# Moving the next step's normalisation, transposes and routing to earlier units in a fused macaron block

## What is computed

```python
x = x + 0.5 * ffn(layernorm(x))
x = x + attention(layernorm(x))
x = x + 0.5 * ffn(layernorm(x))

def ffn(x):                                   # x: tokens x 128
    scores = sigmoid(x @ router_w.T)          # 16 experts in 4 groups
    s = scores + bias
    # the 2 groups with the largest sum of their two best s, in them the 4 best experts
    tw = 2.5 * scores[chosen] / (scores[chosen].sum() + 1e-20)
    h, u = x @ gate_w[e], x @ up_w[e]         # every expert e, F = 128
    y = (silu(h) * u) @ down_w[e]
    return sum_e(combine[:, e] * y[e]) + shared(x)   # shared: two more such products

def attention(x):                             # 32 heads of 4, softmax-free
    q, k, v = split(x @ Wqkv_w.T + Wqkv_b)
    ctx = (q @ k.T) @ v                       # per head
    ctx = groupnorm(ctx per head over time and head dim) * gn_w + gn_b
    return ctx @ out_w.T + out_b
```

## Time and profile before

| | |
|---|---|
| median of 3 runs | 751.8 us (751.61 to 751.99) |
| profiled execution, its own time | 755.5 us |
| its span | 753.8 us |
| mean granted clock of TensorE | 0.965 |
| instructions | 12004 |

### The profile page before, as it was taken

One profiled execution on the slowest core, in us unless ns is written; L12 is line 12 of the kernel. 1 busy time (PEld: TensorE's weight loads), 2 busy tenths in 40 slices (PEclk: granted clock), 3 DMA queues, 4 the chain that ended last, 5 costly groups with the idle time before them and its releaser, 6 DMA issues.

```text
span 753.8 us, 12004 instructions
## 1 busy us (share of the span) xinstructions
PE 680.1 (90%) x3116; PEld 555.4 (74%) x3116; DVE 592.5 (79%) x1571; ACT 397.6 (53%) x784; POOL 432.1 (57%) x373
## 2 busy tenths in 40 slices
PE   3498989989898988989979989799897999989897
PEld 2287778878787877778867878678686878878675
DVE  3898696878887697886878878878788797878674
ACT  3464645555573543755436554366553655555453
POOL 4555655666673553855547455475553766666564
PEclk9799999999998998999989999899998999999999
DMA  6640606041230601405006051050410606041240
GB/s 189 191 168 2 224 1 225 1 180 46 98 129 0 225 2 31 195 0 224 0 5 221 0 194 45 3 223 14 174 65 0 225 15 225 15 168 72 66 174 15
DMA packets 30789, 76.37 MB, mean 101 GB/s; under 512 B 3968, under 2 KB 12688, under 8 KB 30736
## 3 DMA queue, kind: packets, MB, share of 16 engines
q1 hardware_dynamic: 30736, 75.81, 28.0%
HBM read 73.18 MB, written 2.62 MB: 101 GB/s over the span
## 4 chain that ended last, share of the span: by engine, by line
PE 33%; DVE 21%; issue 20%; POOL 18%; DMA 4%; ACT 2%; POOLq 1%; SPq 0%; DVEq 0%; ACTq 0%
POOL A_lo L323 16%; DVE T L952 6%; DVE A L974 5%; PE gateP L410 4%; PE gateP L412 3%; PE gateP L411 3%; PE yP L410 3%; PE yP L411 3%; PE yP L412 3%; PE upP L412 3%; PE upP L411 3%; PE upP L410 3%; DMA CB<-combT 2%; DVE wsum L841 2%; DMA ebias<-in_L_ffn_bias_dram 1%
## 5 line engine op out<-in xcount | busy, mean ns | idle before, releaser
L323 POOL TENSOR_TENSOR A_lo<-A,A_hi 128x512 fp32r<-128x512 f32 x288 | 371.5, 1295 | 252.7 <-ACT A_hi L673 252.6
L656 ACT ACTIVATE gateP<-gateP 128x512 f32<-128x512 f32 x256 | 149.0, 582 | 232.1 <-PE gateP L412 231.6
L952 DVE TENSOR_TENSOR T<-gateP,CB 128x512 f32<-128x512 f32 x256 | 175.3, 685 | 103.9 <-ACT gateP L656 81.1
L673 ACT CAST A_hi<-A 128x512 fp32r<-128x512 f32 x288 | 176.6, 613 | 42.6 <-DVE A L974 42.6
L974 DVE TENSOR_TENSOR A<-upP,T 128x512 f32<-128x512 f32 x256 | 177.0, 691 | 9.1
L410 PE MATMUL gateP<-XT_hi,W_hi 128*128 128x512 f32 x288 | 124.6, 433 | 3.5 <-DVE T L952 3.1
L410 PE MATMUL yP<-A_hi,W_hi 128*128 128x512 f32 x288 | 115.0, 399 | 1.5 <-ACT YT L589 0.9
L410 PE MATMUL upP<-XT_hi,W_hi 128*128 128x512 f32 x288 | 115.5, 401 | 0.3
L412 PE MATMUL gateP<-XT_lo,W_hi 128*128 128x512 f32 x288 | 115.4, 401 | 0.0
L411 PE MATMUL gateP<-XT_hi,W_lo 128*128 128x512 f32 x288 | 115.3, 400 | 0.0
L412 PE MATMUL upP<-XT_lo,W_hi 128*128 128x512 f32 x288 | 114.6, 398 | 0.0
(11 more groups left out here) (169 smaller groups left out, 671.6 us busy)
## 6 DMA issues: line engine op xcount, KB each, us to landing
CB<-combT SPq DMA_DIRECT2D x128, 512.0 KB, 7.1
out_dram<-X SPq DMA_DIRECT2D x8, 256.0 KB, 2.0
X<-in_L_attn_x_dram SPq DMA_DIRECT2D x3, 512.0 KB, 6.1
W_in<-in_L_ffn_gate_w_dram SPq DMA_DIRECT2D x4, 256.0 KB, 5.3
W_in<-in_L_ffn_up_w_dram SPq DMA_DIRECT2D x4, 256.0 KB, 5.3
W_in<-in_L_ffn_down_w_dram SPq DMA_DIRECT2D x4, 256.0 KB, 5.4
X<-in_L_attn_x_dram SPq DMA_DIRECT2D x2, 256.0 KB, 3.7
combT<-CT SPq DMA_DIRECT2D x16, 32.0 KB, 1.8
```

The lines of the kernel that those rows point to most:

```text
L323: pool.tensor_tensor(A_lo[:, slot, :], A[:, slot, :], A_hi[:, slot, :].bitcast(F32), ALU.subtract).then_inc(low_done, 1)
L656: act.activation(dst, gateP[u % 2][:, :], ACT.Silu).then_inc(silu_done, 1)
L673: act.copy(A_hi[:, v % SLOTS, :], A[:, v % SLOTS, :]).then_inc(high_done, 1)
L952: dve.tensor_tensor(T[:, u % TS, :], gateP[u % 2][:, :], CB[:, e, :], ALU.mult).then_inc(gate_weighted, 1)
```

## The change

The preparation is spread over two steps. `stats`, `step_rstd`, `normalise` and `transpose_next` of a step stand at units 12, 13, 14 and 16, and 17 of the step before the preceding one (so they are for step t+2 while step t runs); `next_full` and `next_high` at unit 0, `next_low` and `logits` at unit 1, `route` at units 2 to 9, `route_silu` at 3, `transpose_weights` at 11 and `copy_weights` at 12 of the preceding step. Step 0 prepares step 1 as before (`early`), and step 2 at its units 12 to 17 besides. `transpose_next` gets a further wait, for the copy of the combine weights out of `prepP`. Of attention the stages move three units forward, with some exceptions: statistics take units 0 to 2 in place of 1 to 4, GpSimd's two powers stand at 3 and 27, the `zb` group goes from 31 to 29, the `WoT` product from 32 to 31, its copy from 33 to 32; units 33 to 35 of VectorE and 34 of TensorE stay.

```diff
 pool (GpSimd)
-                    if w == 1 and not (last and s == 1):
-                        step_rstd(2 * p + s + 1)
-                    if w == 7 and not (last and s == 1):
+                    early = first and s == 0
+                    if early and w == 1:
+                        step_rstd(1)
+                    if w == 13 and not last:
+                        step_rstd(2 * p + s + 2)
+                    if w == (7 if early else 1) and not (last and s == 1):
                         next_low(2 * p + s + 1, (s + 1) % 2)
-                    if attention and u == 5:
+                    if attention and u == 3:
...
-                    if attention and u == 30:
+                    if attention and u == 27:

 pe (TensorE)
             def transpose_next(t):
                 pe.wait_ge(xn_ready, 2 * (t + 1))
+                if not (isinstance(t, int) and t == 0):
+                    pe.wait_ge(ct_ready, t)
...
+                    early = first and s == 0
+                    if early and w == 5:
+                        transpose_next(1)
                     if not (last and s >= 1):
-                        if w == 5:
-                            transpose_next(t0 + s + 1)
-                        if w == 7:
+                        if w == (7 if early else 1):
                             logits(t0 + s + 1)
-                        if w == 16:
+                        if w == (16 if early else 11):
                             transpose_weights(t0 + s + 1)
+                    if w == 17 and not last:
+                        transpose_next(t0 + s + 2)
 pe attention: units 12, 15, 16, 19, 21, 23, 26, 29, 32 become 9, 12, 13, 16, 18, 20, 23, 26, 31

 act (ScalarE)
+                    early = first and s == 0
+                    if early and w in (2, 3):
+                        normalise(1, 1, w - 2)
                     if not (last and s >= 1):
-                        if w in (2, 3 if first and s == 0 else 4):
-                            normalise(t0 + s + 1, 2 * ((p + s) % BATCH) + (1 - s), (w - 1) // 2)
-                        if w == 6:
+                        if w == (6 if early else 0):
                             next_high(t0 + s + 1, (s + 1) % 2)
-                        if w == 9:
+                        if w == (9 if early else 3):
                             route_silu(t0 + s + 1)
-                        if w == 17:
+                        if w == (17 if early else 12):
                             copy_weights(t0 + s + 1)
+                    if w in (14, 16) and not last:
+                        normalise(t0 + s + 2, 2 * ((p + 1) % BATCH) + s, w // 2 - 7)
 act attention: units 7 to 10, 13, 16, 22, 33 become 4 to 7, 10, 13, 19, 32

 dve (VectorE)
+                    if early and w == 0:
+                        dve.wait_ge(x_rest, 16 * BATCH)
+                        stats(1, 1)
                     if not (last and s == 1):
...
+                        at = 6 if early else 0
+                        if w == at:
+                            next_full(t0 + s + 1)
+                        if at + 2 <= w < at + 10:
+                            route(t0 + s + 1, w - at - 2)
+                    if w == 12 and not last:
+
+                        dve.wait_ge(mul_done, n + u + 1)
+                        stats(t0 + s + 2, 2 * ((p + 1) % BATCH) + s)
 dve attention: units 1 to 4, 14, 17, 20, 24, 27, 30, 31 become 0 to 2, 11, 14, 17, 21, 24, 27, 29
```

More of the change, by code:

```diff
@@ L449, in attention_stage @@
                 v = ATT_OPS * b
-                if u == 12:
+                if u == 9:
                     pe.wait_ge(xa_ready, b + 1)
@@ L456, in attention_stage @@
                     mm.then_inc(att_pe, 1)
-                if u in (12, 15):
-                    g = (u - 12) // 3
+                if u in (9, 12):
+                    g = (u - 9) // 3
                     if g == 0:
@@ L467, in attention_stage @@
                     mm.then_inc(att_pe, 1)
-                if u == 16:
+                if u == 13:
                     pe.wait_ge(att_act, 6 * b + 1)
@@ L474, in attention_stage @@
                               start=True, stop=True).then_inc(att_pe, 1)
-                if u == 19:
+                if u == 16:
                     pe.wait_ge(att_seq, v + 8)
                     pe.matmul(attP[:, 0:P], WkT[:, :], P1[:, :], start=True, stop=True).then_inc(att_pe, 1)
-                if u == 21:
+                if u == 18:
                     pe.wait_ge(att_seq, v + 10)
@@ L482, in attention_stage @@
                               start=True, stop=True).then_inc(att_pe, 1)
-                if u == 23:
+                if u == 20:
                     pe.wait_ge(att_act, 6 * b + 5)
                     pe.matmul(attP[:, 0:P + 1], Am[:, :], Gc[:, :], start=True, stop=True).then_inc(att_pe, 1)
-                if u == 26:
+                if u == 23:
                     pe.wait_ge(att_seq, v + 12)
@@ L489, in attention_stage @@
                               start=True, stop=True).then_inc(att_pe, 1)
-                if u == 29:
+                if u == 26:
                     pe.wait_ge(att_seq, v + 14)
@@ L493, in attention_stage @@
                               start=True, stop=True).then_inc(att_pe, 1)
-                if u == 32:
+                if u == 31:
                     pe.wait_ge(att_seq, v + 19)
@@ L615, in attention_stage @@
             def attention_stage(u, b):
-                if 7 <= u < 11:
-                    if u == 7:
+                if 4 <= u < 8:
+                    if u == 4:
                         act.wait_ge(att_pow, 3 * b + 2)
-                    for j in range(2 * (u - 7), 2 * (u - 6)):
+                    for j in range(2 * (u - 4), 2 * (u - 3)):
                         ins = act.activation(XA[:, j, 0:P], X[:, bass.ds(b * BT + j, 1), :]
@@ L623, in attention_stage @@
                                              scale=arstd[:, j:j + 1], bias=ashift[:, j:j + 1])
-                    if u == 10:
+                    if u == 7:
                         ins.then_inc(xa_ready, 1)
-                if u == 13:
+                if u == 10:
                     act.wait_ge(att_pe, 12 * b + 1)
                     act.copy(GS[:, :], attP[:, 0:P + 1]).then_inc(att_act, 1)
-                if u in (13, 16):
-                    g = (u - 13) // 3
+                if u in (10, 13):
+                    g = (u - 10) // 3
                     act.wait_ge(att_pe, 12 * b + 2 + g)
                     act.copy(XAT[:, g * TILES:(g + 1) * TILES, :], backP[:, :]).then_inc(att_act, 1)
-                if u == 22:
+                if u == 19:
                     act.wait_ge(att_pe, 12 * b + 6)
@@ L636, in attention_stage @@
                     act.copy(Am[:, :], attP[:, 2 * P:3 * P]).then_inc(att_act, 1)
-                if u == 33:
+                if u == 32:
                     act.wait_ge(att_pe, 12 * b + 10)
@@ L856, in attention_stage @@
                 v = ATT_OPS * b
-                if 1 <= u <= 4:
-                    j0 = 2 * (u - 1)
-                    if u == 1:
+                if u < 3:
+                    if u == 0:
                         dve.wait_ge(x_updated, 2 * b + 2)
-                    for j in (j0, j0 + 1):
+                    for j in range(3 * u, min(3 * u + 3, BT)):
                         ins = dve.bn_stats(ast[:, j, :], X[:, bass.ds(b * BT + j, 1), :]
                                            .rearrange("p o d -> p (o d)"))
-                    if u == 4:
+                    if u == 2:
                         ins.then_inc(att_seq, 1)
                         merge_stats(att_seq, v, ast, anmean[:, :], avar[:, :], aparts)
-                if u == 14:
+                if u == 11:
                     dve.wait_ge(att_act, 6 * b + 1)
@@ L885, in attention_stage @@
                                              ALU.mult, ALU.add).then_inc(att_seq, 1)
-                if u == 20:
+                if u == 17:
                     dve.wait_ge(att_pe, 12 * b + 5)
@@ L899, in attention_stage @@
                                       ALU.add).then_inc(att_seq, 1)
-                if u == 27:
+                if u == 24:
                     dve.wait_ge(att_seq, v + 12)
@@ L914, in attention_stage @@
                                       ALU.add).then_inc(att_seq, 1)
-                if u == 31:
+                if u == 29:
                     dve.wait_ge(att_pow, 3 * b + 3)
@@ L958, in pair @@
                     w, s = u % UNITS, u // UNITS
-                    if w in (13, 14) and not (last and s == 1):
-                        dve.wait_ge(route_seq, ROUTE_OPS * (t0 + s + 1) + (21 if w == 13 else 22))
+                    early = first and s == 0
+                    if w in ((13, 14) if early else (7, 8)) and not (last and s == 1):
+                        dve.wait_ge(route_seq, ROUTE_OPS * (t0 + s + 1) + (21 if w in (7, 13) else 22))
                     dve.wait_ge(silu_done, n + u + 1)
```

6 lines of the change are left out of this document (3 added, 3 removed).

## The result

The changed kernel takes 739.9 us (median of 4 runs, 739.06 to 740.61), the kernel before 751.9 in the same session: a ratio of 0.984 (95% interval 0.982 to 0.986), 12.0 us less. Forecast were 717 us and a range of 706 to 731. The sign was right, the gain a third of the forecast one. The profiled execution takes 739.06 us with a span of 737.3, where the sum gave 718.8.

The account below looks back on a forecast made before the run. VectorE's lag, making TensorE wait, was taken as the bound, with half clock behind `zb` waits. 60.3 us gone against 25.3 new gave net -35.0, from 751.8 to 716.8, say 717 us; range 706 to 731.

Parts of the forecast that it names:

- Attention, first step: First step of each attention pair: VectorE's lag stays below 4.8 up to unit 17, the 2.89 us `comb` wait goes.
- recurrence of D: VectorE's lag (A's end after TensorE's first gate matmul): old + extra + 1.36 - unit length; above 4.76 us TensorE stands.
- The loop's top: Steps 6, 8 and 10: new 1.3 us wait for the logits, replacing some 1.0 us of lag in units 2 to 4.
- step 0: Routing stays at units 8 to 15, statistics come on top at unit 12: longer wait for `comb`, +1.5 us.
- the second attention steps: New waits of about 4.0 us in three pieces from unit 28 on replace one of 4.19; half clock goes.
- Plain steps: The 2.05 us `comb` wait goes, about 0.65 us before unit 12 replaces it: 39.5 us instead of 41.0.
- D(10): Plain step, VectorE's lag at unit 10, after routing part 7: 5.4 us.
- CB: Loads start six units earlier: step 15's late transfer, costing TensorE 1.35 us, is gone; no waits after step 1.
- C: Clock falls in second attention steps all the same, 4 x 2.4 to 3.4 us, once or twice more: 729; chance 0.20.
- B: New waits are hidden too, `wsum` or the `zb` group meeting idle GpSimd: some 6 of 25.3 stay, 698; chance 0.08.
- E: Units 11 and 12 of each step: TensorE stands longer, clock falls to 1.2 GHz every time: 768, slower; chance 0.04.
- D: The wait moves: 1 us more in each of 15 steps, 732; with 4 us at the loop top 740; chance 0.13.

Follow-up runs that it names:

- e1: The changed kernel with GpSimd's split made for one column instead of 512 from unit 4 on: 704.8 us, ratio 0.936 to the kernel before.
- e3: The changed kernel with VectorE's hardware loop over pairs 2 to 5 written out: 729.9 us, ratio 0.967 to the kernel before.
- e5: The changed kernel without the addition of 1e-20 to `wsum`: 737.1 us, ratio 0.979 to the kernel before.
- e7: The changed kernel with only the preparation of the next steps moved, attention's stages where they stood before: 756.1 us, ratio 1.003 to the kernel before.
- e8: The changed kernel with only attention's stages moved, the preparation where it stood before: 766.8 us, ratio 1.017 to the kernel before.

## Why the prediction was wrong

**The step that failed** is "Attention, first step": "D stays below 4.8 up to unit 17". The prediction shows no working for it, and its recurrence of D took each operation's length from the kernel before. In the changed kernel D is 4.9 at units 3 and 4, just over the bound, and then 7.0 and 7.2 at units 5 and 6, because two operations of 0.17 us last 1.26 and 1.31. In the kernel before, most of the routing stood in the gaps of the splits. At D near 3.3 a split begins at 647.03, 649.07 and 651.11 (1.3 us each) and routing part 2 runs from 650.27 to about 651.0, between two of them; in the changed kernel it runs into the row of three, and no gap is left. That GpSimd's power would hold the splits back is not in the prediction either. The lengths were no property of the operations but of their place, and 1.14 against 0.17 us of `wsum` had shown it.

The sizes, against the 18.5 us by which the span is off: step 4, where no loop top comes in, takes 45.9 us instead of 42.0, and 42.8 without collisions (e1); steps 6, 8 and 10 take 47.9 instead of 43.7, and 45.0 without. So collisions make some 12 us of it. The loop's top makes 2 to 3, what is left of the four first steps 2, step 0 with the start some 1, the second attention steps 1.

**The term that was mis-sized** is the loop's top, 1.3 us in steps 6, 8 and 10. The wait for the logits was there as forecast, but 1.71 us and more, since the jump now leaves VectorE idle for 3.0 to 3.2 us where it was 1.94. Steps 6, 8 and 10 are 2.0 to 2.1 us longer than step 4, which has no top, so the term is 2 us short over the three; by e3, which saved 2.7 us in each, it is 4 us short. Why the same loop became dearer stays open.

**What held.** Plain steps: 39.7 us against 39.5, D(10) 5.6 against 5.4, statistics and normalising covered, no wait for `comb`. In place of the 2.05 us stands this wait in the changed kernel's step 13 at unit 12:

```profile
639.04 0.33 PE L450 MATMUL prepP<-ident,comb 128*128 128x128 f32 x1
639.60 0.50 PE L413 MATMUL gateP<-XT_hi,W_hi 128*128 128x512 f32 x1 [0.22 <-DVE T L961]
```

Unit 11 takes 2.9 us from gate to gate, 0.86 over a free unit where some 0.65 were forecast; a bracket counts idleness only from a matmul's modelled end. The second attention steps: waits in three pieces, 0.38, 1.37 and 0.94 us of idleness at units 30, 32 and 33, and 47.2 us against 46.6 to 47.6. Of `zb`'s group in the changed kernel's step 7:

```profile
366.63 1.22 DVE L929 TENSOR_TENSOR gms<-gmean,gsc 128x1 f32<-128x1 f32 x1
367.77 1.38 DVE L930 TENSOR_SCALAR ATs<-AT,gsc 128x128 f32<-128x128 f32 x1
...
369.98 0.49 PE L501 MATMUL attP<-WoT,ATs 128*128 128x128 f32 x2 [1.37 <-DVE zb L937]
```

CB: no wait from step 2 on. Step 0: 58.5 us for 56.5, longer as forecast (1.5), with half clock behind its wait. Two readings of the prediction are loose, without weight in the result: from 660.82 to 663.31 are 2.49 us, not 2.43, and the distances of two A less 1.36 hold idle time of VectorE too, so they are upper bounds of what a routing part costs.

**The rivals.** C, half clock in the second attention steps: no in the profiled execution, 1.00 with three waits in 8 us. The Trainium skill ("TensorE: Matmul & The Clock Gate", "What's actually happening") gives recent activity as what lifts the half rate; the row of waits did not drop it here. The forecast was lucky in this, for the length of a wait alone does not settle the clock: behind the loop's top of step 6 TensorE waits 1.71 us for XT both in the changed kernel and in e5, and the clock stays at 1.00 in the one and falls to 0.50 in the other, where it falls in steps 8 and 10 too. That wait of e5, and the stretches behind it, e5 first and then the changed kernel (columns as in the earlier trace rows):

```profile
292.87 1.07 PE L444 MATMUL prepP<-RT,XT 128*128 128x16 f32 x8 [1.71 <-DVE XT L756]
```

```profile
293.90:299.90 6.00, 6.00 (x21) 4.74 (x21) 5.13 (x20) 3.05 (x8) 3.54 (x4) 0.72 0.00 1
```

```profile
294.70:300.70 6.00, 6.00 (x28) 4.85 (x27) 5.37 (x20) 4.10 (x9) 3.75 (x4) 1.00 0.01 1
```

B: no. E: no. D named the mechanism, a longer operation under a split, and even its time (732, or 740 with a dearer loop top), but put it into all 15 steps and gave it 0.13. It struck in attention's first steps, twice over, so that 740 meets 739.9 is in part luck. That `top` and `mid` end with their splits is a wait for the rest of GpSimd's instruction, not a slowdown by a share. The Trainium skill ("SBUF — State Buffer", "SBUF: two separate sides") states just this: the port pair that VectorE and GpSimd share is an exclusive lock, and whichever instruction starts first keeps it to its end, with VectorE's instructions of two SBUF inputs or in a 2-port mode on the one side. For the splits the runs agree. The prediction had read only that the two contend; this rule belonged into its own recurrence: an operation of that kind that is reached under a split costs the rest of the split.

## What to carry to other kernels

When work on VectorE is moved against a rhythm of GpSimd's instructions, give each small operation on SBUF operands two prices, its own and the rest of the instruction it may fall under, and redo them wherever the lag changes; a lag that grows can move more of them under a split and so feed itself. Look also at what may hold the other engine back: a split that waits behind an instruction of its own engine comes later, together with the next ones, and leaves no gap. Moves that hand a wait from one reader to the next can be worth nothing one by one: e7 and e8 alone were no gain and a loss. Ahead of a rearrangement it pays to run once with the other engine's instruction shrunk, which shows in one number what the collisions are worth.

## What the runs showed of the hardware

- In the changed kernel 35 small operations of VectorE behind unit 4 of step 0 last 1.08 to 1.38 us, in the kernel before 27 of 1.04 to 1.38, and every one ends within 0.15 us of the end of a GpSimd split of 128x512. They have two SBUF inputs, or are a `tensor_scalar` from SBUF to SBUF. The end lies behind the split's by about the operation's own work: 0.01 to 0.05 us for 1 to 32 columns, 0.08 for 128 (`ATs`), and 0.55 for the 128x512 additions `X<-X,Mf`, four of which last 1.11 us for 0.68. The reverse holds too: no operation of two SBUF inputs that began inside a split, by more than 0.05 us, ended more than 0.1 us before it. T and A (one input in PSUM, 0.69 us) are never longer, nor are the statistics (0.28), `reciprocal` (0.18 us from 318.48, inside a split), reductions and maxima, which have one SBUF input and run inside splits at their own length. Under GpSimd's power of 128x8 (1.64 us from 300.38) `score` and `sel` with two SBUF inputs keep 0.22 us, so it is not every GpSimd instruction. By the rule of the Trainium skill ("SBUF — State Buffer", "SBUF: two separate sides") `score` would have waited for the power's end at 302.02; it ran from 301.56 to 301.78, so here row and rule differ, as far as a row of GpSimd tells its length.
- At the top of VectorE's loop the engine is idle for 1.9 us in one program and 3.0 to 3.2 in the other, with the same instructions ahead of it; written out, in the changed kernel, the next A starts with no idleness at all.
- The same wait of TensorE, 1.71 us at the same place of the same stream, left the granted clock at 1.00 in the changed kernel and was followed by 0.50 in e5.
